# Two feed-forward halves with routed experts: the second router keeps its rows on chip, its shared expert is computed among the pairs of experts

## The reference, cut to what matters

```
su = x_flat @ w_shared_up                  # 512 -> 2 x 128
y_s, g_s = split(su)
shared = (silu(g_s) * y_s) @ w_shared_down # 128 -> 512
scores = sigmoid(x_flat @ w_gate)          # 64 experts
w, topk_idx = top 6 of scores, w / sum(w)
pos = place of a row in its expert, at most 256 rows each
h_r = silu(g_r) * v_r                      # per expert, 512 -> 2 x 64
routed = sum over the row's 6 of w * (h_r @ w_down)
ffn = shared + routed
```

## Time and profile before

| what | value |
|---|---|
| median of 3 runs | 3268.29 us (3266.97 to 3268.96) |
| the profiled execution's own time | 3288.66 us |
| its span | 3286.9 us |
| busy: PE | 2812.6 us, 86% |
| busy: DVE | 2045.0 us, 62% |
| busy: ACT | 1481.8 us, 45% |
| busy: POOL | 2210.8 us, 67% |
| mean granted clock of TensorE | 0.926 of full speed |
| moved by DMA | 576.36 MB, mean 175 GB/s |

### The profile page before, as it was taken

The page is one execution under the profiler, slowest core; times in us unless marked ns, Lnnn a source line. Parts: engine busy times, 40 slices in busy tenths (PEclk is TensorE's granted clock), DMA queues, the critical chain, the costliest instruction groups (busy, mean ns, idle before and its releaser), DMA issues. The chain is left out here.

```text
span 3286.9 us, 50812 instructions
## 1 busy us (share of the span) xinstructions
PE 2812.6 (86%) x15136; PEld 1579.5 (48%) x15136; DVE 2045.0 (62%) x3940; ACT 1481.8 (45%) x2815; POOL 2210.8 (67%) x1392
## 2 busy tenths in 40 slices
PE   7967778398899999999999999999999798777760
PEld 4644444176555454555554544455554355444430
DVE  7943222267788787788787877777875397222222
ACT  3422222153666565566565655665656243222210
POOL 2148888462688787788887877877878222788870
PEclk9989887699999999999999999999999898879885
DMA  6479999894577676676776766757766243999998
GB/s 215 167 210 249 235 243 232 191 278 158 113 161 142 136 159 140 142 153 131 166 142 135 159 138 139 156 116 155 144 124 142 89 166 116 245 235 245 235 197 315
DMA packets 217011, 576.36 MB, mean 175 GB/s; under 512 B 33948, under 2 KB 34972, under 8 KB 192792
## 3 DMA queue, kind: packets, MB, share of 16 engines
q0 software_dynamic: 87296, 343.98, 52.0%
q1 hardware_dynamic: 125208, 220.55, 20.5%
q10 hardware_dynamic: 4224, 8.39, 0.7%
HBM read 230.94 MB, written 155.24 MB: 117 GB/s over the span
## 5 line engine op out<-in xcount | busy, mean ns | idle before, releaser
L1716 DVE TENSOR_REDUCE attention_mx<-attention_pM 128x1 f32<-128x512 f32 x1984 | 1210.8, 680 | 208.7 <-PE attention_pM L1575 192.6
L1520 ACT ACTIVATE attention_prob<-attention_pS 128x512 f32<-128x512 f32 x2048 | 1035.0, 631 | 565.9 <-PE attention_pS L1562 471.3
L1461 POOL TENSOR_TENSOR attention_pair<-attention_prob 128x1024 f32<-128x1024 f32 x380 | 949.5, 2507 | 195.6 <-ACT attention_prob L1520 184.0
L1562 PE MATMUL attention_pS<-attention_qT,prep_kT 128*128 128x512 f32 x2048 | 842.0, 417 | 25.3 <-issue 16.7
L1575 PE MATMUL attention_pM<-prep_kT,attention_qT 96*128 96x512 f32 x1984 | 808.3, 410 | 0.0
L1562 PEld LDWEIGHTS attention_pS<-attention_qT,prep_kT 128*128 128x128 f32 x2048 | 389.2, 191 | 365.8 <-issue 178.0
L1600 PE MATMUL attention_pO<-attention_prob,attention_v 128*32 128x512 f32 x4096 | 492.5, 598 | 0.0
L629 POOL DMA_INDIRECT sum<-experts_res,c_table x256 | 403.7, 1577 | 106.7 <-issue 76.6
L1575 PEld LDWEIGHTS attention_pM<-prep_kT,attention_qT 96*128 96x128 f32 x1984 | 378.5, 192 | 110.4 <-DVE attention_mx L1716 44.4
L755 DVE TENSOR_SCALAR experts_res<-experts_pD,experts_rows 128x512 f32<-128x512 f32 x128 | 90.7, 747 | 422.5 <-DMA sum<-experts_res,c_table 277.3
L658 PE MATMUL experts_pT<-c_ident,experts_rows 128*128 128x128 f32 x1024 | 186.3, 325 | 189.9 <-issue 69.4
(11 more groups left out here) (161 smaller groups left out, 2695.2 us busy)
## 6 DMA issues: line engine op xcount, KB each, us to landing
prep_acc<-attention_pair POOLq DMA_DIRECT2D x96, 1024.0 KB, 7.7
attention_acc<-attention_pair POOLq DMA_DIRECT2D x90, 1024.0 KB, 7.6
experts_wup<-in_L_ffn_w_up_dram SPq DMA_DIRECT2D x128, 256.0 KB
attention_qT<-q_parts SPq DMA_DIRECT2D x96, 256.0 KB
xn_rows<-route_xn SPq DMA_DIRECT2D x16, 1152.0 KB, 6.7
sum<-route_sh SPq DMA_DIRECT2D x16, 1024.0 KB, 4.4
experts_wdn<-in_L_ffn_w_down_dram SPq DMA_DIRECT2D x64, 256.0 KB
q_parts<-prep_acc SPq DMA_DIRECT2D x64, 256.0 KB, 4.4
```

What stands on the lines that cost most here:

```text
L1461: pool.tensor_tensor(to[:, part], prob[2 * n % PROBS][:, part], prob[(2 * n + 1) % PROBS][:, part], ALU.add).then_inc(s_pair, 1)
L1520: act.activation(prob[t % PROBS][:, h * QT:(h + 1) * QT], pS[:, at, :], ACT.Exp).then_inc(s_ex, 1)
L1562: pe.matmul(pS[:, at, :], kT[:, key:key + P], qT[g][:, h, :], start=True, stop=True).then_inc(s_sc, 1)
L1716: dve.tensor_reduce(mx[:, unit, part:part + 1], pM[:, r % RING, :], X, ALU.max).then_inc(s_mr, 1)
```

## The change

In both routers:
- `normalise` moves from VectorE to ScalarE, as one activation `xn = rstd * x + shift` for each tile. POOL makes `shift = -mean * rstd` with two more small operations behind its power. On ScalarE the four activations of turn i+1 come behind the copy of the counts of turn i-1; the values of the one-hots (`valued`) come behind the shared expert's sigmoid, the scores' sigmoid behind those.
- On VectorE the places and half of the one-hots of turn i-1 come before the shared expert's products of turn i, the other half behind them.

In the second router alone (`kept` is given):
- the transposed rows go to `kept`, 64 KB in each partition, that lives until the end; the shared expert is left out here, and SP fills `sums[1]` with zeros in its place.

In the second experts stage:
- 16 units of 256 rows of the shared expert are computed out of `kept`: two ahead of pair 0, then one ahead of every second pair. A unit takes the slot of a pair in the buffers `pU`, `sg`, `gs`, `hid` and `pD`. Its result, halved by ScalarE and VectorE, is written over its own rows in `kept`. SP loads `wsu` and `wsd` ahead of the experts' weights.

In the combine VectorE adds `kept` to the first sum, then the second sum.

```diff
@@ route, gpsimd, rsqrt @@
...
+                    pool.tensor_tensor(mean[:, i % 2, :], mv[:, i % 3, :, 0], rstd[:, i % 2, :], ALU.mult
+                                       ).then_inc(s_rd, 1)
+                    pool.wait_ge(s_rd, A + 2 * i + 2)
...
+                    pool.tensor_scalar(shift[:, i % 2, :], mean[:, i % 2, :], -1.0, None, ALU.mult).then_inc(s_rs, 1)
@@ route, scalar @@
+                def normalise(i):
+                    act.wait_ge(s_rs, A + i + 1)
...
+                        act.activation(xn[:, i % RING, j, 0:C], xt[i % XB][:, j, :], ACT.Identity,
+                                       scale=rstd[:, i % 2, j:j + 1], bias=shift[:, i % 2, j:j + 1]).then_inc(s_xn, 1)
...
                     if comes(i - 1):
                         copy_places(i - 1)
+                    if comes(i + 1):
+                        normalise(i + 1)
+                    if comes(i) and kept is None:
+                        sigmoids(i)
+                    if comes(i - 1):
                         valued(i - 1)
                     if comes(i):
-                        sigmoids(i)
+                        scores(i)
@@ route, vector @@
-                    if comes(i + 1):
-                        normalise(i + 1)
                     if comes(i + 2):
                         moments(i + 2)
-                    if comes(i):
+                        variances(i + 2)
+                    if comes(i - 1):
+                        place(i - 1)
+                        one_hots(i - 1, range(2))
+                    if comes(i) and kept is None:
                         gated(i)
-                    if comes(i + 2):
-                        variances(i + 2)
-                    if comes(i):
                         hidden(i)
                     if comes(i - 1):
-                        place(i - 1)
-                        one_hots(i - 1)
+                        one_hots(i - 1, range(2, TURN))
                     if comes(i):
                         select(i)
@@ route, sync @@
+                        sp.dma_start(half_view[i, :, :, :], zero[:, 0:C].unsqueeze(1).to_broadcast([P, TURN, C])
+                                     ).then_inc(s_so[i % 2], 16)
@@ experts @@
+        def units_to(e):
+            return min(2 + e // 2, UNITS)
+        def pairs_to(u):
+            return 2 * max(u - 1, 0)
+        def place(e):
+            return e + units_to(e)
...
+                def unit_up(u):
+                    n = u + pairs_to(u)
...
+                    pe.wait_ge(s_hid, A + n - 1)
+                    for v, o in enumerate((HS, 0)):
+                        for c in range(CK):
+                            t = pe.matmul(pU[n % 2][:, v, :], wsu[:, c, o:o + HS], kept[:, u, c, :], start=c == 0,
+                                          stop=c == CK - 1)
...
+                def unit_down(u):
...
+                    for h in range(HALVES):
+                        pe.matmul(pD[:, h, h, :], hid[n % 2][:, h * P:(h + 1) * P], wsd[:, :], start=True, stop=True
+                                  ).then_inc(s_sd, 1)
...
+                for n in range(PAIRS + UNITS + 1):
+                    e, u = item(n)
+                    old_e, old_u = item(n - 1)
+                    if e is not None:
                         gathered(e)
+                    if old_e is not None:
+                        down(old_e)
+                    if old_u is not None:
+                        unit_down(old_u)
+                    if e is not None:
                         up(e)
+                    if u is not None:
+                        unit_up(u)
@@ combine, vector @@
+                    dve.wait_ge(s_g[0][i], A + 16)
+                    dve.tensor_tensor(all_tiles, all_tiles, own, ALU.add).then_inc(s_two, 1)
+                    dve.wait_ge(s_two, A + i + 1)
+                    dve.wait_ge(s_g[1][i], A + 16)
                     dve.tensor_tensor(got[i][0][:, :, :], got[i][0][:, :, :], got[i][1][:, :, :], ALU.add
```

234 lines of the change are left out of this document (150 added, 84 removed).

## The result

| | runs | us, median (lowest to highest) | ratio to before, 95% interval |
|---|---|---|---|
| before | 4 | 3268.62 (3266.97 to 3271.05) | |
| with the change | 4 | 3228.39 (3227.14 to 3230.82) | 0.9873 [0.9860, 0.9885] |

The change takes 40.2 us off; 44.6 were predicted. The profiled execution of the changed kernel took 3228.58 us (span 3226.7), 0.2 us from its median.

A forecast was written before the change was run, and what follows sets the result against it. It took VectorE's stretched normalisation to bound router turns and POOL's chain the second experts. First router -8.6, second router -39.0, second experts +3.0, combine 0 sum to -44.6 us: 3223.7 us for the median, range 3207 to 3248.

The forecast's parts named there:

- Part 1, turns: First router: with VectorE relieved of normalising, TensorE's 19.5 us become the period over six turns, 10.1 us less.
- VectorE keeps up: First router: after the relief VectorE has some 17 us of work in a 19.5 us turn, so it does not bound.
- Part 1, head: First router's start: added POOL operations and slower ScalarE activations are not hidden, 1.5 us more, estimated between 0 and 3.
- Part 2, turns: Second router: without normalising and the shared expert, seven turns at 15.9 us, 33.6 us less.
- Part 2, head: Second router's start: without the shared expert's matmuls the first top-8 comes earlier, 5.4 us less.
- Part 3: Second experts: 14 units hide under POOL's adds, the two ahead of pair 0 do not; 3.0 us more.
- +32.7 without stalls: Second experts: first add 32.7 us after SP's first issue if nothing stalls; 5 us of stall were added, giving +37.7.
- The 20.4 us: Whole kernel: profiled execution's excess over the median; the predicted difference was carried over, 3244.1 us profiled and 3223.7 median.
- Half clock in the second router: Rival: TensorE wholly at 1.2 GHz makes second-router turns 16.6 us, seven times 1 us more, 3231 us; chance 0.12.
- Experts start late: Rival: the two units ahead of pair 0 cost the second experts 14.6 us instead of 3, 3235 us; chance 0.13.
- Units not hidden: Rival: second experts' pair results miss POOL behind units; +27 us, or +77 and 3301 us at clock 0.75; chance 0.05.
- VectorE and POOL shut each other out: Rival: second router's one-hots meet both added POOL operations, 0.8 us a turn for 0.3, 3227 us; chance 0.09.

The follow-up runs named there:

- c_before2: The kernel before, unedited, run again for its profile in the job of the last four runs: 3269.9 us (one execution).
- c_after2: The changed kernel, unedited, run again on the same chip as c_before2: 3229.6 us, ratio to before 0.9875.
- e3_order: The changed kernel with both routers' lists back in the old order, ScalarE still normalising: 3272.3 us, ratio to before 0.9948.
- c_before: The kernel before, unedited, run again with a profile: 3288.6 us, ratio 0.9993.
- e2_kept: The kernel before plus only the kept rows and shared-expert units; VectorE normalising, lists in old order: 3291.3 us, ratio to before 1.0005.
- e9_kept2: The same program as e2_kept, run again on another chip: 3260.7 us, ratio to before 0.9974.
- e7_both: The changed kernel with no unit ahead of pair 0 and turn 0 normalised on VectorE in both routers: 3222.0 us, ratio to before 0.9851.
- c_after: The changed kernel, unedited, run again in another job: 3230.2 us, ratio to before 0.9874.
- e5_none: The changed kernel with the shared expert left out of the second FFN altogether, so no units: 3221.5 us.
- e8_hold: The changed kernel with POOL's gathers from pair 2 on held until pair 0's up-projection is done, both experts stages: 3245.9 us.
- e1_act: The kernel before plus only ScalarE normalising and the new list order in both routers; no kept rows: 3266.2 us, ratio to before 0.9930.
- e4_later: The changed kernel with no shared-expert unit ahead of pair 0, the first coming behind pair 1: 3229.3 us.

## Why the prediction was right, by its own steps

The mechanism held: VectorE's stretched normalisation was the cost of the second router and, once the lists were reordered, of the first, and the new bounds were the two that were named. The forecast was 4.7 us too low, well inside its range of 3207 to 3248. But it was nearer than its terms: those of the first router miss by 5.3 us one way and by 4.2 the other, and that these cancel is luck. By stage, c_before2 against c_after2 (same chip, both at their usual level), spans 3268.1 and 3227.1:

| step | predicted | measured |
|---|---|---|
| first router, turns | -10.1 | -15.4 |
| first router, head | +1.5 | +4.7 |
| second router, turns | -33.6 | -34.2 |
| second router, head | -5.4 | -1.1 |
| tails of the two routers, behind the last top-8 | 0 | +1.0, -0.7 |
| second experts | +3.0 | +6.3 |
| combine | 0 | +0.2 |
| first experts and attention | 0 | +0.9, -2.7 |
| sum | -44.6 | -41.0 |

**Part 1, turns: right in kind, too small.** The period was to be TensorE's 19.5 us and is 18.7, once 17.6, and the seventh, "at 19.5 already", fell to 18.7 too. The 19.5 was the length of a turn, and the work in it 18.83; TensorE, once it is the bound, has no gaps. "VectorE keeps up, it has some 17 us of work": it has 18.46 of 18.70 us, since POOL's product now stretches `route_ve` by 2.0 us. The cover was 0.24 us and not 2.5. That the new order of the lists is needed for this term at all, the prediction said only in passing; e3_order shows that it is all of the term.

**Part 1, head: the step that failed.** 1.5 us was an estimate between 0 and 3, and it is 4.7. It counted the added operations of POOL and ScalarE, and the start of the shared product is indeed 1.9 us later. The rest is the speed of the product behind it, 6.43 us in c_after2 and 3.70 in c_before2; the prediction put this at nothing, as in the profile that it read the product took 3.70 us. It was slow in all eight profiles with ScalarE at the head and in two of the six with VectorE (c_before, e2_kept), so what decides it is open.

**Part 2, turns: right to 0.6 us, by the mechanism given.** The places wait for POOL's product 9.1 us behind the top-8, the moments fill that wait, and a turn is 9.1 + 1.8 + 4.7 us and the rest. VectorE waits for POOL only in turns without moments, as said.

**Part 2, head: the other step that failed.** Against the first profile of the kernel before the head gained 3.6 us (27.7 to 24.1), against its second 1.1 (25.2 to 24.1), for 5.4 predicted. Taking the shared product out alone did give as much: 5.4 us from c_before2's 25.2 to e9_kept2's 19.8, and 5.9 on the other chip, from c_before's 27.7 to e2_kept's 21.8. Normalising turn 0 on ScalarE takes back about 2: 21.8 to 23.9 from e2_kept to e3_order on one chip, and 1.7 from e7_both's 22.1 to c_after's 23.8. The other 2 stand beside TensorE's clock. The gate matmuls took 3.79 us in e9_kept2 and 7.09 in every other kernel that keeps the rows, e2_kept, which is the same program, and e7_both, which normalises turn 0 on VectorE, among them. So the half clock is there with either engine, and against c_before2, whose head had the full clock, it eats the gain. The prediction saw a half clock in the head and took it for a part of the product that was to go; it allowed "7.0 at 1.2" for the gate and then counted 3.5. TensorE's timeline and busy times in the first profile of the changed kernel:

```profile
2586.94 1.94 PE L315 MATMUL route_pT<-c_ident,route_xn 128*128 128x128 f32 x8 [0.70 <-ACT last_kept L408]
2589.57 7.09 PE L332 MATMUL route_pSc<-route_wg,last_kept 128*128 128x64 f32 x32 [0.69 <-ACT last_kept L408]
...
2592.00:2595.00 3.00, 3.00 (x16) 3.00 (x15) 0.00 (x0) 1.61 (x2) 0.00 (x0) 0.50 0.88 337
```

7.09 us at a granted clock of 0.50 (1.2 GHz); before them TensorE stood 0.69 us twice, between its short groups of transposes.

**Part 3: the path was right, its base was not.** "+32.7 without stalls" measured +32.0. But the prediction added 5 us for the stall that the earlier trace rows showed, and set the sum against a kernel before that had the stall as well. At the level of the medians neither has it: the first add of the kernel before comes 27.95 us after SP's first issue (2777.12 to 2805.07), so the head of the stage costs 4.0 us. By the table's mark it is 4.1 in the first profile of the changed kernel and 4.7 in c_after2 (34.4 and 29.7). The rest of the 6.3 is 1.3 between the first and the last add and 0.3 behind it, which the prediction had at nothing. Otherwise the units behind pair 0 are hidden: POOL's pairs follow each other at 12.63 us in the changed kernel, as before at 12.60.

**The 20.4 us** between the profiled execution and the median were taken over as an offset. They were no offset: some 14 of them were idle stretches at the starts of the two experts stages, one of which the sum had a term for. By c_after2 that is worth 1.7 of the 3.3 us by which part 3 is off (4.7 at the head for 3.0); the other 1.6 are those behind the first add.

**The rivals.** *Half clock in the second router*: the clock did fall. Three turns in TensorE's busy times:

```profile
2612.74:2628.70 15.96, 11.28 (x64) 10.66 (x65) 15.75 (x58) 8.28 (x14) 4.65 (x4) 0.61 0.63 216
2628.70:2644.62 15.92, 11.93 (x110) 10.61 (x108) 15.71 (x58) 10.08 (x18) 4.65 (x4) 0.97 0.61 200
2645.00:2661.00 16.00, 11.70 (x68) 11.06 (x69) 15.79 (x59) 7.89 (x13) 4.64 (x4) 0.57 0.62 211
```

At 0.57 to 0.61 a turn takes what it takes at 0.97, because VectorE is busy for 15.7 of it. The rival needed the whole turn at half clock, and even at 0.57 that isn't reached. (Its price was also too high: by its own 16.6 and 15.9 us a turn would cost 0.7 more, not 1.) *Experts start late*: not at the level of 3270 us; at 3290 e2_kept and e3_order show 7 to 8 us of it. *Units not hidden*: not at 3270, where e5_none bounds all of them at 5.9 us. At 3290 the two kernels lose 9 to 10 us between the first and the last add, so there the rival is open. At 3269 the granted clock over the middle of the stage rose from the 0.86 of the earlier trace rows to 0.98, so TensorE gained where it got more work:

```profile
2762.00:3130.00 368.00, 329.26 (x1984) 206.65 (x1980) 129.54 (x224) 102.46 (x180) 294.29 (x228) 0.98 1.01 234
```

*VectorE and POOL shut each other out*: the added POOL operations cost nothing that shows, since a turn is within 0.1 us of the forecast. But the exclusion itself is there in the turns: four normalisations at 4.79 us beside the product (e9_kept2) and 1.91 in the head, and `route_ve` at 2.20 us beside it. This agrees with the rule of the Trainium skill (SBUF — State Buffer, "Who interferes with whom").

**What stays open.** What makes the idle stretches. They came with the level for the kernel before (two profiles with, one without), and so did the pauses of POOL in the middle of the stage for the two kernels with units. The changed kernel was profiled twice more and never at 3290, and e8_hold neither; whether it would gain 40 us there, or some 30 (e3_order's 17 and the 12 of the order), isn't known. Why TensorE's clock is at one level in one head and at the other in the next is open as well. Nor was it tried which of the two new orders, ScalarE's or VectorE's, the first router needs.

## What to carry to other kernels

Where an elementwise operation of VectorE is long beside an operation of POOL and short elsewhere, move it to another engine and look for what takes its place in line; moved without reordering what the new engine owes the old one, it gained nothing here in one router (e3_order) and 12 us with the order (e1_act). A steady state and its head can want different engines: ScalarE is right for turns 1 to 7 and VectorE for turn 0, which was worth 6 us of the two routers from e4_later to e7_both, 3 of them by the speed of one product, which may not come each time. And if the profiled execution is slower than the median, take a second profile before subtracting: the excess sits in a place, and terms read from that place are wrong.
